# A graph network kernel on one core: TensorE's loop written out, and one small product per group taken out

## What is computed

```python
x = _layernorm(x + L0(x, adj, adj, bias))     # out = (adj*adj)^T x + bias, per batch
x = _layernorm(x + L1(x, adj, W_lang, W_grav, W_V, W_O, gate, log_sigma))
# L1:
z_l, z_g, v = h @ W_lang.T, h @ W_grav.T, h @ W_V.T
A_l = max(cosine(z_l, z_l), 0) * not_eye          # 64x64 per batch
A_g = exp(-dist2(z_g, z_g) / (2 sigma^2)) * not_eye
K   = w * row_normalised(A_l * mask) + (1 - w) * row_normalised(A_g * mask)
out = (K @ v) @ W_O.T
```

## Time and profile before

| | before |
|---|---|
| median of 3 runs | 571.79 us (570.57 to 572.08) |
| the profiled execution: time, span | 572.66 us, 570.9 us |
| mean granted TensorE clock, as a share of full speed | 0.991 |
| ACT, POOL busy (share of the span) | 392.6 us (69%), 211.0 us (37%) |
| matmuls and weight loads recorded | 6536 and 6536 |
| DMA, all queues | 66.07 MB, mean 116 GB/s |

### The profile page before, as it was taken

One profiled execution on the slowest core, in us unless ns is written; L12 is line 12 of the kernel. 1 busy time (PEld: TensorE's weight loads), 2 busy tenths in 40 slices (PEclk: granted clock), 3 DMA queues, 4 the chain that ended last, 5 costly groups with the idle time before them and its releaser, 6 DMA issues.

```text
span 570.9 us, 16726 instructions
## 1 busy us (share of the span) xinstructions
PE 544.7 (95%) x6536; PEld 289.8 (51%) x6536; DVE 461.1 (81%) x1009; ACT 392.6 (69%) x794; POOL 211.0 (37%) x230
## 2 busy tenths in 40 slices
PE   9998699999999999999999999999999999998893
PEld 7543444545454545546454545455454545454361
DVE  1675778889797979798998979797979889896645
ACT  1577745777868778777887786877877776636362
POOL 0132453525344253635243433526363525122021
PEclk9999899999999999999999999999999999999998
DMA  8763344472635445553736354554556333525003
GB/s 261 211 141 78 74 89 98 69 202 50 179 78 142 106 101 147 119 147 82 184 64 184 64 159 89 130 119 110 147 109 158 74 121 54 143 30 146 22 2 147
DMA packets 98430, 66.07 MB, mean 116 GB/s; under 512 B 73696, under 2 KB 77792, under 8 KB 98400
## 3 DMA queue, kind: packets, MB, share of 16 engines
q1 hardware_dynamic: 98400, 65.66, 47.3%
HBM read 21.27 MB, written 16.78 MB: 67 GB/s over the span
## 4 chain that ended last, share of the span: by engine, by line
PE 81%; SPq 8%; DVE 5%; DMA 3%; issue 1%; ACT 1%; POOL 0%; POOLq 0%; ACTq 0%
PE proj L543 18%; PE proj L501 15%; PE ps_t L557 8%; PE ps_k L543 7%; PE proj L513 6%; PE ps_k L501 5%; SPq L361 5%; PE ps_k L513 4%; PE front L460 3%; PE ps_v L572 2%; PE ps_t L581 2%; PE ps_t L633 2%; PE front L633 2%; PE ps_t L513 2%; SPq L372 1%
## 5 line engine op out<-in xcount | busy, mean ns | idle before, releaser
L1435 POOL TENSOR_TENSOR x_lo<-x_in,x_hi 128x512 f16<-128x512 f32 x60 | 71.2, 1189 | 142.3 <-ACT x_hi L781 142.3
L543 PE MATMUL proj<-m_hi,ht_hi 128*64 128x512 f16 x384 | 73.8, 381 | 0.0
L543 PE MATMUL proj<-m_lo,ht_hi 128*64 128x512 f16 x384 | 73.4, 379 | 0.0
L543 PE MATMUL proj<-m_hi,ht_lo 128*64 128x512 f16 x384 | 73.4, 379 | 0.0
L1050 DVE TENSOR_TENSOR p_lo<-proj,p_hi 128x512 f16<-128x512 f32 x96 | 60.6, 683 | 10.4 <-ACT p_hi L791 10.4
L513 PE MATMUL proj<-ht_turn,l_turn 64*64 64x512 f16 x432 | 68.1, 379 | 0.0
L791 ACT ACTIVATE p_hi<-proj 128x512 f16<-128x512 f32 x96 | 51.6, 594 | 21.0 <-PE proj L513 21.0
L785 ACT ACTIVATE h_hi<-h 128x512 f16<-128x512 f32 x64 | 40.0, 630 | 36.5 <-DVE h L1030 36.2
L1465 POOL TENSOR_TENSOR t_diag<-t_sb,eye 128x512 f32<-128x512 f32 x15 | 24.0, 1597 | 92.8 <-ACT t_sb L802 92.8
L557 PE MATMUL ps_t<-ht_hi,p_hi 128*128 128x64 f16 x512 | 48.5, 196 | 5.5 <-DVE p_lo L1050 5.5
L557 PEld LDWEIGHTS ps_t<-ht_hi,p_hi 128*128 128x128 f16 x512 | 46.0, 100 | 12.2 <-issue 12.2
(11 more groups left out here) (278 smaller groups left out, 1658.3 us busy)
## 6 DMA issues: line engine op xcount, KB each, us to landing
x_in<-in_x SPq DMA_DIRECT2D x32, 512.0 KB, 7.1
out<-o SPq DMA_DIRECT2D x15, 1024.0 KB, 5.1
ht_turn<-ht_hi SPq DMA_DIRECT2D x16, 192.0 KB, 2.8
ht_turn<-ht_lo SPq DMA_DIRECT2D x16, 192.0 KB, 2.8
ht_turn<-ht_hi SPq DMA_DIRECT2D x16, 128.0 KB, 2.4
ht_turn<-ht_lo SPq DMA_DIRECT2D x16, 128.0 KB, 2.6
w_raw_lang<-in_L_gnn_W_lang SPq DMA_DIRECT2D x4, 256.0 KB, 3.1
o<-in_L_gnn_W_O SPq DMA_DIRECT2D x1, 1024.0 KB, 8.8
```

The source lines that it names most:

```text
L543: mm = pe.matmul(value_bank[p][q * N:(q + 1) * N, :], a[g.parity][:, k, rows:rows + N], b[:, k, :], start=(n == 0), stop=(n == len(passes) ...
L1435: pool.tensor_tensor(x_lo[:, p, :], x_in[g.parity][:, p, :], x_hi[:, p, :], ALU.subtract).then_inc(xlo_ready, 1)
```

## The change

`run` gets an argument `unrolled`. TensorE passes it, and its twelve groups of the loop are then emitted one after the other, with constant wait counts; the other engines keep their loops. The product of ones in `attend_gate` is gone; its waits stay, and now stand ahead of the first product of `attend`.

```diff
-        def run(engine, iteration, back):
+        def run(engine, iteration, back, unrolled=False):
 
             iteration(Group(0, 0), has_prev=False, has_next=True, has_split=True, has_square=True)
-            with engine.Fori(0, G // 2 - 2) as i:
+            def two(i):
                 iteration(Group(i, 1), has_prev=True, has_next=True, has_split=True, has_square=True)
                 iteration(Group(i + 1, 0), has_prev=True, has_next=True, has_split=True, has_square=True)
+
+            if unrolled:
+                for i in range(G // 2 - 2):
+                    two(i)
+            else:
+                with engine.Fori(0, G // 2 - 2) as i:
+                    two(i)
...
                 if nxt:
                     pe.wait_ge(y_ready, nxt.count(4, 4))
-                pe.matmul(ps_v[:, 0:1], ones16[:, :], ones16[:, 0:1], start=True, stop=True, skip_group_check=True)
...
-            run(pe, iteration, back)
+            run(pe, iteration, back, unrolled=True)
```

## The result

The kernel after takes 574.11 us in the median (571.51 to 575.98, 20 runs), the kernel before 571.32 us (568.95 to 574.18, 20 runs beside it): a ratio of 1.0047, 95% interval 1.0031 to 1.0062, so some 2.7 us slower. The forecast was a change of +0.6 us and a time of 572.4, so it lies 1.7 us too low, and the result is outside the likeliest case's own range of 570.1 to 573.6. The wide range of 568.0 to 576.5, which was drawn to reach rival (b), holds it.

A forecast was written before the change was run, and what follows sets the result against it. TensorE's list was taken to bound the kernel. Product -3.2, loop 0, pages on SyncE's queue +1.2, on the load of x +2.6, stores 0: +0.6 us, 573.3 on the profiled execution, median 572.4, range 568.0 to 576.5.

The forecast's parts named there:

- likeliest case: Whole kernel: the product's gain and the page costs about cancel, 570.1 to 573.6 us; chance 0.36.
- rival (b): Slower: instruction pages delay the load of x, Gram products wait about half a microsecond each time; 575.6 us, chance 0.31.
- What bounds the kernel: TensorE, busy 95%, runs its list end to end; time off its list comes off the total unless others come late.
- The product of ones: TensorE ahead of the attends: removal saves 0.24 us a group, waits free; -3.2 us, bounds -3.6 and -2.0.
- It stays so without the product of ones, since both ends move: Slack of 0.42 us between DVE's last `p_lo` and the Gram products, claimed unchanged when the product goes.
- The loop: TensorE's six jumps are hidden behind queued matmuls, so removing them gains 0, bounds 0 and -0.1 us.
- Pages on the SyncE queue: Instruction pages lengthen SyncE's transposes and turn copies, TensorE waits for the turn: +1.2 us, bounds 0 and 4.
- Pages on the load of x: Pages land x 0.9 us late, delaying the Gram products; nine groups at 0.3 us: +2.6 us, bounds 0 and 8.
- (a): Instruction page fetches are hidden, leaving only the product's gain: 568.6 us; chance 0.32.
- (c): Loop jumps cost what the profile can't show; unrolling gives back six page fetches of about 1 us: 562.6 us, chance 0.01.
- (d): First attend product, carrying the waits, still starts 0.1 us late; gain only 2.0, time 573.6 us; chance within the likeliest case's 0.36.

The follow-up runs named there:

- second: TensorE's loop written out but the product of ones kept, against the kernel before: 574.51 us, ratio 1.0040.
- third: Kernel after, with SyncE issuing the load of x ahead of the store instead of behind it: 570.54 us, ratio 0.9976 to the kernel before.
- fifth: Kernel after, but three of TensorE's six loop passes kept (groups 1 to 6) and groups 7 to 12 written out: 572.10 us, ratio 1.0017 to the kernel before.
- fourth experiment: Kernel after, with GpSimd's `t_diag` also waiting until DVE's `h_lo` is done: 572.53 us, ratio 1.0012 to the kernel before.

## Why the prediction was right or wrong

The runs let the change be walked in steps, each a ratio: product away in the loop 0.9930, then written out with x early 0.9976, then x late again 1.0047.

| step | predicted, us | measured, by ratios, of 571.8 us | measured, groups 3 to 12 |
|---|---|---|---|
| product of ones away | -3.2 | -4.0 (-5.3 to -2.7) | -2.35 |
| written out, x early (pages on SyncE's transposes and turns) | +1.2 | +2.6 (+0.9 to +4.4) | +3.17 |
| x late again (pages on the load of x) | +2.6 | +4.1 (+2.6 to +5.5) | +2.83 |
| sum | +0.6 | +2.7 (+1.8 to +3.5) | +3.65 |

In the other order, writing out with the product kept costs +2.3 us (+1.2 to +3.4), and taking the product away then brings +0.4 (-1.0 to +1.8): the steps do not add up on their own, and the table books what they share with the pages.

- **The number**: a little slower was forecast (+0.6) and measured (+2.7), but the sum adds a term that holds in the loop alone (-3.2) to two page terms that were too small (+3.8, for a measured +6.7 without the product). That the wide range holds the result is owed to the bound for (b), whose mechanism did not happen.
- **What bounds the kernel**: right. TensorE's list end to end, and every tenth of a microsecond taken off it shows if nobody is late (308.68 busy in 308.68).
- **The product of ones**: right in size (0.235 a group) and in that the waits are free on the attend. What was wrong is to add it to the page terms as if they did not touch. "It stays so without the product of ones, since both ends move" holds for the Gram products, but not for the landing of x, which is fixed by the queues: against `t_diag` the slack shrinks by up to the 0.23 us saved. In the written out kernel, x late, the product's going is worth nothing that the medians show.
- **The loop**: right, 0. In the half-looped kernel the looped groups take 30.87 us and so does group 7, written out and without a wait.
- **Pages on the SyncE queue**: the step that failed. The prediction priced only the turn ("two on transposes are nearly covered"). The first projection, which waits for the transposes themselves, was left out of the sum, and in the kernel after it is the larger one. Groups 3 to 12 took 314.68 - 308.68 = 6.00 us more than without pages; 2.58 of that stand in the parts with the projections (3.15 with x first), for the +1.2. First projections that start late are 1.66 of the 2.58 (0.55, 0.60, 0.26 and 0.25 in four groups). The room at the first projection is 0.84 us, and I had never read it.
- **Pages on the load of x**: right that x is late, low in the size (3.40 us in the second parts of groups 3 to 12, for the +2.6), wrong in the place. That the gaps at `spread` add up to 2.64 us is luck. The Gram products waited twice, 0.14 and 0.02 us; the price is asked further down, at `spread`, through the order of `h_lo` and `t_diag`. The lead of `h_lo` over `t_diag` was 0.2 us before and 0.02 to 0.23 without the product, less than the 0.42 that was measured to the Gram products. I looked for the slack at the next wait of TensorE and stopped there.
- **The rivals**: (b) is the nearest, with the slower side and the load of x; its mechanism, Gram products waiting, is not what happens. (a) is refuted by the second, third and fifth experiments. The Trainium skill (Runtime: NRT & Kernel Launch, Instruction fetch mechanics) calls the cost of crossing a page boundary mostly hidden. This case agrees for the engine that fetches (group 7 of the half-looped kernel has three pages and takes 30.87 us) and not for the DMAs beside it (transposes of up to 2.50 us). (c) is refuted by the second, which is slower than the kernel before with no jump left; (d) by the 0.43 us of the trace after.
- **The profiled execution's own time**: it rose by 0.9 us only, for the medians' 2.7, since the ends of the two executions differ by the clock and by one wait.

## What to carry to other kernels

In this kernel unrolling a loop that fetched no page while it ran bought nothing, since the engine is paced by its work, and it put a stream of instruction pages beside the kernel's own DMAs, which made 19 of the 28 transposes that met one up to 1.2 us longer, with 0.84 us of room behind them: keep the loop and take only the product out (568.39 us, 0.9930). Slack must be followed past the next wait of the bounding engine, down to where two engines race for a port, since there a third of a microsecond turned the order, cost 1.3 us on DVE and 0.7 on TensorE. Two edits that each look at their own slack may share it: price them together.

## What the runs showed of the hardware

- A GpSimd product and a DVE product of 128x512 that overlap: DVE's takes 0.68 us when it starts 0.09 us ahead, 1.76 us when it starts 0.25 us behind. Holding GpSimd back by a wait removed all of the long ones (fourth experiment).
- Of 28 DMA transposes of 1.27 us beside which a page was fetched, 19 took 1.40 to 2.50 us; 84 without a page took at most 1.28 (the kernel after).
- The same wait of 2.8 us on TensorE is followed over the next ten microseconds by a mean granted clock of 0.70 to 0.85 in seven of the ten profiled executions and of 1.00 in three. A wait of 2.3 us in the middle of one of them was followed by 0.57 over four microseconds, one of 1.8 us by 1.00.
